# Rows of the tap matrices 18 floats apart instead of 20 in a depthwise 5x5 convolution on TensorE

## The reference

```python
k = jnp.transpose(kernel, (1, 2, 0))[:, :, None, :]
y = lax.conv_general_dilated(x, k, window_strides=(1, 1), padding='SAME',
        dimension_numbers=('NHWC', 'HWIO', 'NHWC'), feature_group_count=ch)
return x + y
```

## The kernel before

| banks | first tile | second tile |
|---|---|---|
| 0 | 11x16 from float 2 (corner) | 11x18 |
| 1, 3, 4 | 13x16 from float 2 | 13x18 |
| 2 | 14x16 from float 2 | 14x18 |
| 5 | 11x16 from float 2 (corner) | 11x18 |
| 6, 7, 10, 11 | 13x18 | 13x16 from float 0 |
| 8, 9 | 11x18 | 11x16 from float 0 (corner) |

## Time and profile before

### The profile page before, as it was taken

How to read it: one execution, slowest core, us unless ns; L and a number is a source line. 1 busy time by engine, 2 the same in 40 slices (tenths; PEclk the granted TensorE clock), 3 DMA queues, 4 the chain that set the end, 5 groups by cost and what they waited for, 6 DMA issues and landing times.

```text
span 804.1 us, 18943 instructions
## 1 busy us (share of the span) xinstructions
PE 790.0 (98%) x6528; PEld 788.7 (98%) x6528; DVE 740.4 (92%) x2116; ACT 669.6 (83%) x1538; POOL 551.1 (69%) x652
## 2 busy tenths in 40 slices
PE   5999999999999999999999999999999999999997
PEld 5999999999999999999999999999999999999997
DVE  5999999999999999999999999999999999999996
ACT  6788888888888888888888888888888888888885
POOL 7758668586676776766858667586676775866851
PEclk9999999999999999999999999999999999999999
DMA  9999999999999999999999999999999999999975
GB/s 359 424 407 379 405 379 370 380 398 379 397 366 377 398 373 400 364 404 367 396 364 398 379 382 378 376 391 379 398 372 403 368 392 380 371 397 379 387 294 234
DMA packets 28752, 304.42 MB, mean 379 GB/s; under 512 B 3185, under 2 KB 3313, under 8 KB 4209
## 3 DMA queue, kind: packets, MB, share of 16 engines
q1 hardware_dynamic: 28656, 303.22, 97.3%
HBM read 153.79 MB, written 149.42 MB: 377 GB/s over the span
## 4 chain that ended last, share of the span: by engine, by line
PE 96%; DVE 2%; POOL 1%; DMA 0%; issue 0%; ACT 0%; DVEq 0%; ACTq 0%
PE sums L385 32%; PE sums L392 28%; PE sums L391 27%; PE sums L388 9%; DVE x_low L330 1%; DVE y_out L341 1%; DMA first<-consts 0%; POOL matrix L284 0%; POOL spread L271 0%; ACT y_out L313 0%; ACT x_high L306 0%; POOL taps L262 0%; POOL spare L259 0%; POOL taps L257 0%; DVEq L144 0%
## 5 line engine op out<-in xcount | busy, mean ns | idle before, releaser
L385 PE MATMUL sums<-matrix,x_low 126*128 126x208 f32 (+5 forms) x2304 | 641.1, 278 | 9.3 <-POOL matrix L284 8.1
L392 PE MATMUL sums<-matrix,x_high 126*128 126x208 f32 (+4 forms) x1920 | 542.3, 282 | 0.0
L391 PE MATMUL sums<-matrix,x_high 126*128 126x208 f32 (+4 forms) x1920 | 540.8, 282 | 0.0
L284 POOL TENSOR_TENSOR matrix<-spread,mask 127x300 fp32r<-127x300 f32 x384 | 382.6, 1027 | 223.2 <-PE sums L392 221.3
L313 ACT ACTIVATE y_out<-sums 128x270 f32<-128x270 f32 (+6 forms) x1152 | 429.6, 392 | 121.2 <-PE sums L392 108.0
L385 PEld LDWEIGHTS sums<-matrix,x_low 126*128 126x128 f32 (+1 forms) x2304 | 443.8, 193 | 9.8 <-POOL matrix L284 8.1
L341 DVE TENSOR_TENSOR y_out<-sums,y_out 128x176 f32<-128x176 f32 (+2 forms) x1728 | 401.3, 275 | 52.9 <-ACT y_out L313 25.2
L330 DVE TENSOR_TENSOR x_low<-x_in,x_high 128x768 fp32r<-128x768 f32 x384 | 401.5, 1046 | 6.0 <-ACT x_high L306 6.0
L392 PEld LDWEIGHTS sums<-matrix,x_high 126*128 126x128 f32 (+1 forms) x1920 | 370.4, 193 | 0.0
L391 PEld LDWEIGHTS sums<-matrix,x_high 126*128 126x128 f32 (+1 forms) x1920 | 369.7, 193 | 0.6
L306 ACT ACTIVATE x_high<-x_in 128x768 fp32r<-128x768 f32 x384 | 321.0, 836 | 8.0 <-DMA x_in<-x 8.0
(11 more groups left out here) (5 smaller groups left out, 0.6 us busy)
## 6 DMA issues: line engine op xcount, KB each, us to landing
x_in<-x SPq DMA_DIRECT2D x95, 1536.0 KB, 10.0
y<-y_out SPq DMA_DIRECT2D x95, 1520.0 KB, 12.7
rest<-later SPq DMA_DIRECT2D x1, 2300.0 KB, 14.2
x_in<-x SPq DMA_DIRECT2D x4, 384.0 KB, 5.2
y<-y_out SPq DMA_DIRECT2D x1, 832.5 KB, 3.4
y<-y_out SPq DMA_DIRECT2D x1, 687.5 KB, 5.0
mask<-masks SPq DMA_DIRECT2D x1, 300.0 KB, 4.1
first<-consts SPq DMA_DIRECT2D x1, 125.0 KB, 2.1
```

The lines of the kernel that those rows point to most:

```text
L284: pool.tensor_tensor(matrix[c % SLOTS][kind][0:whole, part, :].rearrange("p (b e) -> p b e", b=ROWS // TAPS), spread[kind][0:whole, part, ...
L385: pe.matmul(target, low, turned[:, HIGH], start=tile is bank["tiles"][0], stop=False, skip_group_check=True)
L391: pe.matmul(target, high, turned[:, LOW], start=False, stop=False, skip_group_check=True)
L392: product = pe.matmul(target, high, turned[:, HIGH], start=False, stop=last, skip_group_check=True)
```

## The change

A row of the tap matrix is 18 floats long in place of 20, a part has 15x18 = 270 cells in place of 300, and the mask has the same form. The spread taps keep rows of 20 floats (a new constant `SPREAD`), of which the products read the first 18. The order of the instructions on every engine is as before, and PE's matmuls have the same shapes; POOL's products have 270 elements each.

In the program that is built, the moving operand of a tile with 18 columns is now one run of 198, 234 or 252 floats, where it was 11, 13 or 14 runs of 18 floats that lie 20 apart. That of a tile with 16 columns has runs of 16 floats, 18 apart. The low part begins 270 floats behind the high part.

```diff
-ROWS, COLS = 15, 20
+ROWS, COLS = 15, 18
+SPREAD = 20
 CELLS = ROWS * COLS
...
-        spread = [sbuf(f"spread{k}", [P, 2, TAPS * COLS], F32) for k in range(KINDS)]
+        spread = [sbuf(f"spread{k}", [P, 2, TAPS * SPREAD], F32) for k in range(KINDS)]
...
-                    shape = [whole, 2 * TAPS, COLS // TAPS, TAPS]
+                    shape = [whole, 2 * TAPS, SPREAD // TAPS, TAPS]
...
-                    shape = [whole, ROWS // TAPS, TAPS * COLS]
+                    shape = [whole, ROWS // TAPS, TAPS, COLS]
                     for part in (HIGH, LOW):
                         pool.tensor_tensor(
-                            matrix[c % SLOTS][kind][0:whole, part, :].rearrange("p (b e) -> p b e", b=ROWS // TAPS),
-                            spread[kind][0:whole, part, :].unsqueeze(1).broadcast_to(shape),
-                            mask[0:whole, kind, :].rearrange("p (b e) -> p b e", b=ROWS // TAPS),
+                            matrix[c % SLOTS][kind][0:whole, part, :].rearrange("p (b d q) -> p b d q", d=TAPS, q=COLS),
+                            spread[kind][0:whole, part, :].rearrange("p (d q) -> p d q", q=SPREAD)[:, :, 0:COLS]
+                            .unsqueeze(1).broadcast_to(shape),
+                            mask[0:whole, kind, :].rearrange("p (b d q) -> p b d q", d=TAPS, q=COLS),
                             ALU.mult).then_inc(matrix_step, 1)
```

## The result

The changed kernel takes 785.9 us in the median of four runs (784.29 to 789.02), against 805.86 (805.76 to 806.24) for the kernel before on the same chip: a ratio of 0.9756, with a 95% interval from 0.9726 to 0.9786. The forecast was 783.0 us, in a range from 777 to 800. The profiled execution took 784.29 us, 782.5 of it span; the one of before 805.91.

What follows compares the result with a forecast made beforehand. The prediction took PE to bound the kernel, at 8.203 us per channel. Its terms summed to about -0.25 us per channel, -22.8 us over 91 channels and -0.2 at the start: 805.91 to 783 us, range 777 to 800.

Steps and rivals of the forecast that it cites:

- The law of the tiles: PE matmuls: four cycles per group of four floats touched plus 28, at least 0.1125 us per load; -0.245 us per channel.
- Item 1: PE's 18-column tiles become one run: 13x18 -0.16 us per channel, 14x18 -0.04, 11x18 0.
- Item 2: PE's 16-column tiles from float 2 touch fewer groups: 13x16 -0.065 us per channel, 14x16 -0.03.
- Item 3: PE's 16-column tiles from float 0 touch more groups, hidden by loads, but lose a head start: +0.05 us per channel.
- Item 4: PE's corner tiles: two gain what two lose, 0, within 0.04 us either way.
- Item 5: POOL's products, 30 elements fewer: -78 ns each, nothing in the steady part, -0.16 us at the start.
- what is late next: After PE: DVE would need 7.93 us per channel against PE's 7.95; DMA would need 392 GB/s.
- a chance of 0.08 to DMA: Rival: DMA becomes the bound, at 384 GB/s a channel takes 8.12 us, 798 us in all; chance 0.08.
- The prediction's own sign of being wrong: In PE's timeline: 13x18 still at 0.36 us, or matmuls at 0.11 us with PE waiting for DVE or ACT.
- DVE as the bound: Rival: DVE sets the pace, 792 us at 8.05 us per channel, 801 at 8.15; chance 0.21.
- The slower rival: DVE's x_low and POOL's products keep disturbing each other and DVE falls behind: 828 to 865 us; chance 0.09.

Runs made afterwards that it cites:

- at 22: Kernel before with tap-matrix rows 22 floats apart: 805.73 us; with a fourth output buffer too 801.42 us, or with POOL multiplying only 18 floats per row 800.81 us.
- a pitch of 19: Kernel before with tap-matrix rows 19 floats apart instead of 20, parts of 288 floats: 791.76 us, ratio 0.9838.
- pitch 21: Kernel before with tap-matrix rows 21 floats apart instead of 20, parts of 316 floats, spread rows of 25: 800.82 us, ratio 0.9938.

## Why the prediction was right, and which size was off

**The law of the tiles: right in sign, place and nearly in size.** Forecast per channel -0.245 us, measured -0.296 (8.203 to 7.907). Term by term, from the table of medians:

- Item 1, 13x18: forecast -0.16, measured 7 x -0.022 = -0.155. 14x18: -0.04 and -0.025. The 11x18 tiles were given 0, and gained 4 x -0.007 = -0.03; why, no run shows.
- Item 2, from float 2: -0.065 and 3 x -0.031 = -0.09; 14x16 -0.03 and -0.034. These tiles end at 335 ns and not at the loads' 337.5.
- Item 3, from float 0: +0.05 and 4 x 0.006 = +0.025; the loads did hide the added groups.
- Item 4, the corners: 0 forecast, and the four together go from 1.210 to 1.214 us.
- Item 5, POOL's products: 798 ns in the median, -36 and not -78; undisturbed (the shortest) 701 for 816 in before, -115. On rows 20 apart it changes nothing in the steady part, as the run with short products alone shows; beside late stores the products' length does count, as at 22. At the start PE's wait for the first matrix fell from 8.1 to 7.7 us.

The floor is seen in the weight loads (PE's loads, start us; answers to the earlier trace rows):

```profile
299.07 0.19 PEld L393 LDWEIGHTS sums<-matrix,x_high 126*128 126x128 f32 x1
...
299.96 0.19 PEld L387 LDWEIGHTS sums<-matrix,x_low 126*128 126x128 f32 x1
```

Eight loads in 0.89 us, 0.111 each, through tiles of 18 and 16 columns alike. Over the steady channels loads follow each other by 0.112 us in the median in 11x18, 13x16 and 13x18 tiles alike. (The loads in the earlier trace rows are those of an 11x18 and a corner tile, not of a 13x16; the pace is the same.) So in most tiles the load of the other operand now sets PE's time. Shorter reads could bring something only in the 14x18 and the corner tiles, which take clearly longer than their loads; no run tries it.

Shown by runs is that the tiles of 16 columns go by the groups touched (the shift by two floats, the pitch of 22), and that POOL's shorter products by themselves bring nothing. That a tile of 18 columns is one long run of 234 floats is not what counts by itself: at a pitch of 19, with gaps between its rows, half of its saving of 22 ns is there already. But what does count in these tiles, more than half of the gain, is not shown: at 18, 19, 20, 21, 22 and 24 floats the 13x18 tile takes 341, 352, 363, 365, 365 and 372 ns. These never fall as the rows move apart, while the group count fits at 18, 20 and 22 alone. The Trainium skill's row on lines (SBUF — State Buffer, section Specifications (TRN2)) says that full bandwidth needs two or more hits on a line of 16 bytes, and also that each cross to a new line pays a penalty. The prediction used the first half alone and took the page to speak against it. That half does not hold for these reads: by it the two kinds of 13x16 tile would have been alike in the kernel with shifted rows, where they differ by 29 ns, as they did in before by 42. With the second half the row agrees with the trace in direction, since the slower kind crosses to more lines, five in a row for four.

**The step that was mis-sized: what is late next.** I compared DVE's need of 7.93 us with PE's 7.95, and gave a chance of 0.08 to DMA, which I weighed as a rate (392 GB/s at the new pace). The rate was no limit: after the change the core moves 390 GB/s, and 393 with four buffers, at the same busy share of 0.99. What ran short was time, not rate. From a store's issue to the end of PE's last matmul in the bank that ACT copies first into the same buffer there were 13.9 us in the median before and 12.7 after. The two channels in between, each 0.3 us shorter, are 0.6 us of that; the rest is that stores are issued later, measured against PE. The stores themselves took 12.7 us in the median before and 13.0 after. So of the stores of channels 5 to 92 seven landed too late before, and 58 after. The nine waits of the earlier trace rows were the sign, and I read their small sum in place of what they stood close to. The prediction's own sign of being wrong, PE waiting for DVE or ACT, came in part. The step cost 5.6 us in the profiled run; with a fourth buffer 6.6 us come back in the median, for 2.0 on the kernel before. This is nearly the same as what the larger gain of the tiles gave (91 x 0.051 = 4.6 us beyond the forecast), so 785.9 stands close to 783 in part because two errors cancel.

**The rivals.** DVE as the bound for the whole run (0.21) did not come: undisturbed channels are PE's. In some channels DVE does end last, behind a late store. The slower rival (0.09) did not happen with shorter products, yet its mechanism is real: with products of 360 cells in place of 270 DVE becomes the chain and 17 us are lost.

## What to carry to other kernels

Look at where the rows of TensorE's moving operand begin and end: here a row of 16 floats that began in the middle of a group of four paid for a group more, so choose the start or the distance so that few half-used groups are left, until the weight loads are the floor. Before a faster stage is counted as gained, take every buffer that is handed on at its pace and compare the time from the start of its transfer to its next use, before and after, with the time that the transfer takes; a busy share does not show this. A few short waits for one transfer can be a sign that a few per cent more speed will turn them into many, as here nine into 54.

## What the runs showed of the hardware

- In these fp32r matmuls the price of reading the moving operand depends on where its rows begin in a group of four floats: the same 126x208 matmul takes a third of 0.327 or of 0.366 us. Read by groups, one shared by two neighbouring rows is paid less than twice (pitch 19), and one of which a row uses a single float less than in full (pitch 21); a price that rises with the distance between rows fits the 13x18 tiles too.
- Loads of the stationary operand (128 columns) follow each other by 0.112 us in the median, whether the matmul between them has 198, 208 or 234 columns.
- The busy share of the DMA engines says little about how near they are to their limit: 0.99 at 380, at 390 and at 393 GB/s.
- DVE's `x_low` of 768 elements takes 0.95 us where POOL is idle and up to 1.7 us beside POOL's products. With rows 24 apart its median is 0.949 us beside products of 270 cells and 1.136 beside 360.
